# A four-layer conditional block on one core: the dense stage on pairs of tiles as seven block products, the preparation reordered, the adapter tables kept in DRAM

## The reference, cut to what matters

```python
x = x + L0(x)   # long convolution per channel with a kernel made from state space parameters, masked by length
x = x + L1(x)   # einsum('bct,bcd->bdt', x, weights[cond])            weights: (16, 64, 64)
x = x + L2(x)   # x @ base_weight.T + bias + (x @ A[adapter].T) @ B[adapter].T      rank 16 of 32 adapters
x = x + L3(x)   # x @ W.T + 0.5 * (x @ lora_A[labeler]) @ lora_B.T                  rank 32 of 5 labelers
```

## Time and profile before

| | us |
|---|---|
| median of three runs | 1658.99 |
| the profiled execution | 1661.53 |
| its span in the trace | 1659.4 |
| PE busy | 1602.0 (97%) |
| DVE busy | 797.9 (48%) |
| POOL busy | 590.8 (36%) |
| ACT busy | 441.5 (27%) |
| mean granted clock of PE | 0.985 of full speed |

### The profile page before, as it was taken

One profiled execution on the slowest core, in us unless ns is written; L12 is line 12 of the kernel. 1 busy time (PEld: TensorE's weight loads), 2 busy tenths in 40 slices (PEclk: granted clock), 3 DMA queues, 4 the chain that ended last, 5 costly groups with the idle time before them and its releaser, 6 DMA issues.

```text
span 1659.4 us, 32019 instructions
## 1 busy us (share of the span) xinstructions
PE 1602.0 (97%) x10317; PEld 1551.0 (93%) x10317; DVE 797.9 (48%) x1502; ACT 441.5 (27%) x751; POOL 590.8 (36%) x769
## 2 busy tenths in 40 slices
PE   6789989999999998899999999999999999999999
PEld 5678879999999997899999999999999999999998
DVE  7861348878887886233333333333333333333332
ACT  3311134454445543111111111111111111111111
POOL 4552136666666665322222222222222222222221
PEclk9889999999999999899999999999999999999999
DMA  9501357666666764323323232322223223222321
GB/s 239 49 7 56 99 178 243 232 235 238 241 233 228 236 240 170 93 88 100 92 92 99 88 100 92 98 94 92 98 89 98 93 93 98 92 95 92 94 97 65
DMA packets 121309, 214.02 MB, mean 129 GB/s; under 512 B 57873, under 2 KB 74909, under 8 KB 118625
## 3 DMA queue, kind: packets, MB, share of 16 engines
q1 hardware_dynamic: 120988, 213.61, 40.2%
q10 hardware_dynamic: 294, 0.05, 0.0%
HBM read 141.41 MB, written 72.20 MB: 129 GB/s over the span
## 4 chain that ended last, share of the span: by engine, by line
PE 59%; POOL 0%; POOLq 0%; issue 0%; ACT 0%; DVE 0%; DVEq 0%
PE ps L1322 47%; PE ps L1296 7%; PE ps L1344 4%; PE ps L1310 1%; PE ps L1304 0%; POOLq L1151 0%; POOL dense L1172 0%; POOL m_gath L1153 0%; ACT dense L1204 0%; POOLq L1159 0%; POOLq L1158 0%; DVE y_out L1275 0%; POOL a_gath L1162 0%; POOL a_gath L1160 0%; POOL m_gath L1139 0%
## 5 line engine op out<-in xcount | busy, mean ns | idle before, releaser
L1322 PE MATMUL ps<-dense,x2t 128*128 128x384 f32 (+1 forms) x4608 | 821.7, 336 | 0.0
L1322 PEld LDWEIGHTS ps<-dense,x2t 128*128 128x128 f32 x4608 | 775.3, 188 | 2.2
L1172 POOL TENSOR_TENSOR dense<-a_gath,dense 128x384 fp32r<-128x384 f32 x128 | 126.4, 1009 | 499.5 <-ACT dense L1204 499.5
L1007 PE MATMUL ps<-toep,ut 128*128 128x512 f32 (+2 forms) x1152 | 228.2, 343 | 0.0
L1007 PEld LDWEIGHTS ps<-toep,ut 128*128 128x128 f32 x1152 | 195.4, 189 | 16.9
L482 POOL TENSOR_TENSOR toep<-toep_raw,toep 128x1024 fp32r<-128x1024 f32 x64 | 152.5, 2383 | 142.1 <-ACT toep L594 142.1
L1218 ACT ACTIVATE y_out<-ps 128x384 f32<-128x384 f32 x64 | 31.4, 490 | 543.7 <-PE ps L1344 543.7
L1296 PE MATMUL ps<-m_gath,x_in 128*128 128x128 f32 x1024 | 128.3, 280 | 13.4 <-DMA x_in<-x_d 9.6
L1296 PEld LDWEIGHTS ps<-m_gath,x_in 128*128 128x128 f32 x1024 | 123.0, 196 | 13.8 <-DMA x_in<-x_d 9.8
L1250 DVE COPY hm<-ps 64x128 f32<-64x128 f32 x64 | 18.1, 283 | 236.7 <-PE ps L1304 236.7
L905 PE MATMUL ps<-p,staged 128*128 128x512 f32 x528 | 123.1, 395 | 8.9 <-DVE dense L626 8.9
(11 more groups left out here) (184 smaller groups left out, 1726.2 us busy)
## 6 DMA issues: line engine op xcount, KB each, us to landing
toep_raw<-kern_d SPq DMA_DIRECT2D x64, 512.0 KB, 4.2
xt<-in_x SPq DMA_DIRECT2D x64, 512.0 KB, 4.9
x_d<-xt SPq DMA_DIRECT2D x64, 512.0 KB, 4.4
x_in<-x_d SPq DMA_DIRECT2D x64, 512.0 KB, 3.6
out<-y_out SPq DMA_DIRECT2D x64, 512.0 KB, 2.7
stack<-b_d SPq DMA_DIRECT2D x130, 128.0 KB, 2.7
stack<-b_d SPq DMA_DIRECT2D x128, 64.0 KB, 2.7
w_raw<-in_L_cond_W SPq DMA_DIRECT2D x8, 512.0 KB, 7.0
```

The lines of the kernel that those rows point to most:

```text
L1007: mm(y[:, half * HB + i * P:(half + 1) * HB], xs[:, a, half * half_t + i, :], tp[:, b, 0:HB - i * P], start=i == a == b == 0, stop=False)
L1172: ins = nc.gpsimd.tensor_tensor(to[:, 1], of, f(to[:, 0]), ALU.subtract)
L1322: ins = mm(outs[g], x2t[v][:, a, i, :], w[:, b, i % half_t, first:end], start=i == a == b == 0, stop=g == 2 and i == K8 - 1 and a == 1)
```

## The change

Three things change.

**The dense stage works on pairs of tiles.** The two tiles of a pair are the two block rows of a 2 x 2 block matrix, the halves of T its block columns; the dense matrix is cut in four 512 x 512 quadrants. Seven products of 512-deep blocks take the place of eight (Winograd's form of Strassen's method). The operands on the x side (a11, a12, a22 and the sums s1 to s4) are made anew for each pair by ACT and DVE; those on the weight side are made once, in the preparation, by DVE and ACT, by sums of quadrants. Four of the products are wide: they carry the 96 adapter columns. A product is 4 chunks x 3 passes, each as two matmuls: 256 and 256 columns, or 256 and 352 columns. The results lie in six PSUM banks; what two results share is accumulated once and read in between. The two tiles' outputs are put together from several PSUM reads.

**Adapter tables.** The tables of adapter columns are no longer in SBUF. The preparation stores them in DRAM (`a2_d`, `a3_d`) and SP loads the rows of each sample: `tab2` and `tab3`, two DMAs a sample, 128 partitions x 512 or 1024 bytes each. DVE makes for the second tile of a pair the difference of the table's halves (`difference`), ACT and DVE the high and low parts.

**The preparation's jobs are reordered.** After d0 and d4 come layer 3's tables, three of the four B jobs, the small products, the convolution kernels and the transposes of layer 2's A; then d1, d5, d2, d6, d3, d7, and the last B job around the transpose of the first channel. The bias row is loaded by ACT's queue at the start. SBUF is laid out anew. The convolution's instructions stay as they are.

The core of the diff:

```diff
@@ preparation: order of PE's jobs
+    ORDER = [(f"t{i}", 1 + i % 3) for i in range(K8)] + [
+        ("d0", 0), ("par", 1), ("d4", 3), ("a3a", 2), ("a3b", 1), ("b2_0", 0), ("b2_1", 3), ("b2_2", 2),
+        ("c", 1), ("row", 0), ("b3", 3), ("k0", 2), ("k1", 1), ("la0", 0), ("la1", 3), ("la2", 2), ("la3", 1),
+        ("d1", 0), ("d5", 3), ("d2", 2), ("d6", 0), ("d3", 1), ("d7", 2), ("b2_3", 3)]
...
@@ dense stage, SP (sync)
+            def pair(n, last_one):
+                if not last_one:
+                    sp.wait_ge(mixed, 4 * n + 4)
+                    for v in range(2):
+                        load_x1(n + 1, v)
+                    a, l = ids(n + 1, B), ids(n + 1, 2 * B)
+                    for v in range(2):
+                        sp.wait_ge(h_lo[v], n + 1)
+                        load_tables(v, a, l)
+                    sp.wait_ge(adapted, 2 * n + 2)
+                    for v in range(2):
+                        load_c(v, a, l)
+                sp.wait_ge(y12_added, n + 1)
+                sp.dma_start(out_rows[bass.ds(2 * n, 1)].squeeze(0), y_out[0][:]).then_inc(y_stored[0], 16)
+                if not last_one:
+                    sp.wait_ge(p_done, n + 1)
+                    for v in range(2):
+                        load_stack(v, a)
+                sp.wait_ge(y21_added, n + 1)
+                sp.dma_start(out_rows[bass.ds(2 * n + 1, 1)].squeeze(0), y_out[1][:]).then_inc(y_stored[1], 16)
...
@@ dense stage, DVE (vector)
+            def difference(n):
+                dve.wait_ge(tab_landed[1], 64 * n + 64)
+                for t in (tab2[1], tab3[1]):
+                    tt(t[:, :, K4:K8], t[:, :, K4:K8], t[:, :, 0:K4], ALU.subtract).then_inc(diffed, 1)
...
+            def pair(n, last_one):
...
+                if not last_one:
+                    difference(n + 1)
+                dve.wait_ge(m2_done, n + 1)
+                h_rows(n, 0)
+                if not last_one:
+                    h_low(n + 1, 0)
+                h_columns(n, 0)
+                dve.wait_ge(m4_done, n + 1)
+                h_rows(n, 1)
...
+                dve.wait_ge(rv_done, n + 1)
+                tt(halves(y_out[0][:, HB:T]), halves(y_out[0][:, HB:T]), of_r, ALU.add).then_inc(y12_added, 1)
+                dve.wait_ge(p_done, n + 1)
+                tt(halves(y_out[1][:, HB:T]), halves(y_out[1][:, HB:T]), of_p, ALU.add).then_inc(y22_added, 1)
+                tt(halves(y_out[1][:, 0:HB]), halves(y_out[1][:, 0:HB]), of_v, ALU.add).then_inc(y21_added, 1)
...
@@ dense stage, PE (tensor)
+            def turn(n, v):
+                pe.wait_ge(hrow_ready, 2 * n + v + 1)
+                ready(pe, hs_lo, 2 * n + v)
+                nc.tensor.transpose(acc[:, SMALL_BANK, 0:P], hrow[v][:], ident[:]).then_inc(turned, 1)
...
+            def pair(n, last_one):
+                pe.wait_ge(a11_lo, n + 1)
+                pe.wait_ge(h_lo[0], n + 1)
+                ready(pe, y22_added, n)
+                product(xa11, M1, PS_SHARED, P_OWN, ALL, True).then_inc(m1_done, 1)
...
+                product(xs1, M5, RV_SHARED, R_OWN, ALL, True).then_inc(m5_done, 1)
...
+                product(xa12, M2, PS_SHARED, S_OWN, ALL, True).then_inc(m2_done, 1)
...
+                product(xa22, M4, RV_SHARED, V_OWN, FRONT, True)
+                turn(n, 0)
+                product(xa22, M4, RV_SHARED, V_OWN, BACK, True).then_inc(m4_done, 1)
+                adapters(n, 0)
+                quarter(n + 1, 0)
...
+                product(xs2, M6, PS_SHARED, P_OWN, FRONT, False)
+                turn(n, 1)
+                product(xs2, M6, PS_SHARED, P_OWN, BACK, False)
...
+                low_rank(0, 0, acc[:, S_OWN, RIGHT], acc[:, PS_SHARED, RIGHT]).then_inc(lr11_done, 1)
+                adapters(n, 1)
+                quarter(n + 1, 1)
...
+                product(xs4, M3, RV_SHARED, R_OWN, ALL, False)
+                quarter(n + 1, 2)
...
+                product(xs3, M7, PS_SHARED, P_OWN, ALL, False).then_inc(m7_done, 1)
+                low_rank(0, HB, acc[:, RV_SHARED, LEFT], acc[:, R_OWN, LEFT])
...
+                low_rank(1, 0, acc[:, V_OWN, RIGHT], acc[:, RV_SHARED, RIGHT]).then_inc(rv_done, 1)
+                pe.wait_ge(u3_copied, n + 1)
+                low_rank(1, HB, acc[:, PS_SHARED, LEFT], acc[:, P_OWN, LEFT]).then_inc(p_done, 1)
+                quarter(n + 1, 3)
```

More of the change, by code:

```diff
@@ L92, in program, with f, wide @@
[L92 to L96, removed]
+    def f(ap):
+        return ap.bitcast(F32)
+    weights, o_fixed = at("weights", [P, 4, BLOCK], F32R, 0)
+    o_w = [4 * BLOCK * i for i in range(4)]
+    def wide(i, half, m):
+        start = (half * 4 + m) * WIDE
+        return weights[:, i, start:start + WIDE]
@@ new lines, in plain, with quadrant @@
+    def plain(i, half, m):
+        start = 8 * WIDE + (half * 3 + m) * HB
+        return weights[:, i, start:start + HB]
+    def quadrant(i, half, m):
+        return wide(i, half, m)[:, D_AT[m]:D_AT[m] + HB]
+    raw_m5, raw_m4, raw_m6, raw_m7 = [], [], [], []
+    for i in range(4):
+        for raws, start in ((raw_m5, (4 + M5) * WIDE + D_AT[M5]), (raw_m4, (4 + M4) * WIDE + D_AT[M4]),
+                            (raw_m6, 8 * WIDE + (3 + M6) * HB), (raw_m7, 8 * WIDE + (3 + M7) * HB)):
+            raws.append(at(f"raw{start}_{i}", [P, HB], F32, o_w[i] + 4 * start)[0])
@@ L110, in program @@
     bias_p3, o = at("bias_p3", [P, K8], F32, o)
[L112 to L133, removed]
+    o = o_w[0]
     def nat(name, cols, dtype=F32, parts=C):
@@ L180, in program @@
[L180 to L189, removed]
+        t, o = at(name, shape, dtype, o)
+        return t
+    xa11, xs1, xa12, xa22 = (place(n, [P, 2, K4, P], F32R) for n in ("xa11", "xs1", "xa12", "xa22"))
@@ L909, in split_job, with chunk_of @@
                 ins.then_inc(job_done, 1)
+            def chunk_of(t, n, c):
+                for half in range(2):
+                    cols = slice(half * HB, (half + 1) * HB)
+                    for a, b in PASSES:
+                        ins = mm(t[:, cols], staged[n % 2][:, a, c, :], p3[:, c, b, cols],
+                                 start=c == a == b == 0, stop=c == K8 - 1 and a == 1)
+                return ins
             def transpose_w3(i):
-                t = job(J_W3 + i)
+                t = job(f"t{i}")
                 pe.wait_ge(w3_ready, i + 1)
@@ L1070, in program @@
+    y11_added, y12_added, y22_added, y21_added = (sem(f"{n}_added") for n in ("y11", "y12", "y22", "y21"))
     PAIRS = TILES // 2
@@ L1224, in _ @@
+            over_pairs(act, pair)
         @block.vector
@@ new lines, in h_rows @@
+            def h_rows(n, v):
+                own, other = ((P_OWN, H_END), (S_OWN, H_FRONT)) if v == 0 else ((R_OWN, H_END), (V_OWN, H_FRONT))
+                parts = []
+                for b in range(2):
+                    rows, cols = slice(b * C, (b + 1) * C), slice(b * R2, b * R2 + R2 + R3)
+                    parts.append((hrow[v][rows, cols], rows, slice(b * (R2 + R3), (b + 1) * (R2 + R3))))
+                first, second = acc[:, own[0], own[1]], acc[:, other[0], other[1]]
+                for b, (to, rows, cols) in enumerate(parts):
+                    ins = nc.vector.tensor_copy(to, first[rows, cols])
+                ins.then_inc(h_part, 1)
+                dve.wait_ge(h_part, 2 * n + v + 1)
+                for to, rows, cols in parts:
+                    ins = tt(to, to, second[rows, cols], ALU.add)
+                ins.then_inc(hrow_ready, 1)
@@ L1347, in tile, with quarter @@
-            def tile(k, v):
-                if exists(k, v + 1):
-                    mixing(k, v + 1)
-                dense(k, v)
-            mixing(0, 0)
-            over_tiles(pe, tile)
+            QUARTERS = ((0, 0), (1, 0), (1, 1), (0, 1))
+            def quarter(n, q):
+                v, half = QUARTERS[q]
+                if half == 0:
+                    pe.wait_ge(x1_landed[v], 16 * n + 16)
+                    pe.wait_ge(gathered[v], n + 1)
+                ready(pe, quarter_read, 4 * n + q)
+                for i in range(K4):
+                    c = half * K4 + i
+                    ins = mm(acc[:, MIX_BANK, i * P:(i + 1) * P], x1_in[v][:, c * P:(c + 1) * P], m_gath[v][:], start=True, stop=True)
+                ins.then_inc(mixed, 1)
```

1205 lines of the change are left out of this document (670 added, 535 removed).

## The result

The changed kernel takes 1870.61 us (median of 4 runs, 1869.19 to 1873.19) against 1659.37 us for the kernel before on the same chip: ratio 1.1273 [1.1253, 1.1292]. It is slower, as predicted; the prediction said 1925 us, 54 us too many. The span is 1868.5 us, the mean granted clock 0.933.

A forecast was written before the change was run, and what follows sets the result against it. PE alone bound the old kernel; the new bound is a ring through SP (19.1 us), DVE (1.9), PE (14.9) and y12's add (1.0): 36.9, with 2.5 clock loss 39.4 a pair. With start, end and preparation: 1925 us, range 1800 to 2010.

The forecast's parts named there:

- SP was to be never idle for long: Dense stage, SP's queue: a sign that would show the prediction right; no size beyond these words.
- PE's leg: PE from turn 0 to `rv_done` in a pair: 14.9 us of work, plus 2.5 us of lost clock.
- the ring: Dense stage: y12 added, SP's loads, DVE, turn 0, PE, y12 added; 39.4 us a pair with clock loss, chance 0.70.
- rival 1: Dense stage: tables land in time, 9.9 us after y12's add, and PE is the bound; 1590 us, chance 0.12.
- two x1 loads and eight reads: SP's queue before the table loads: 0.9 us for the loads and 6.4 (5.7 to 8.4) for the `value_load`s.
- landing: Table rows arriving after SP's last table load: 2.8 us, 2.7 as the stack's 128 KB, up to 3.6 as x1.
- DVE from landing to the transpose: DVE's `difference` and four small `h_rows` copies with hand-overs, before turn 0: 1.9 us.
- clock loss: PE behind 9 us of idle time before each turn 0: 2.5 us more a pair, bounds 0 and 3.
- rival 2: Dense stage: the tables' wait holds in each pair but PE's clock stays up; 1850 us, chance 0.10.
- Rival 3: SP's queue: released at the mixing's end rather than by y12's add; 1780 us, chance 0.05.
- Rival 4: PE's seven products don't save, 256-column pairs costing more in alternating banks; 10% more is +45 us, chance 0.02.
- The 0.4 us for which M1 was to wait for y22's add: Pair's end: `y22_added` comes 1.7 us after `rv_done`, next M1 due at 1.3; costs only if tables don't hold PE.

The follow-up runs named there:

- e2: The changed kernel with each pair's eight stack loads issued by GpSimd instead of SP: 1806.2 us, ratio 1.088.
- e3: The changed kernel with SP's eight reads of table numbers made twice in each pair: 2009.88 us, ratio 1.2107.
- e4: The changed kernel with 44 unused 256-column matmuls added on PE before turn 0 in each pair: 1839.91 us, ratio 1.1083.
- e8: The changed kernel with 56 unused 256-column matmuls added on PE before turn 0 in each pair: 1820.91 us, ratio 1.0980.
- e1_late: The changed kernel with the next pair's table work moved behind this pair's adapter copies on VectorE and behind two reads on ScalarE: 1594.37 us, ratio 0.9609.
- e5_dve: The changed kernel with only `difference` moved, on VectorE, behind `h_columns(n, 1)`; ScalarE's order kept: 1835.85 us, ratio 1.1071.
- e9_dve2: The changed kernel with `difference` and `h_low(n + 1, 0)` both moved behind `h_columns(n, 1)` on VectorE, ScalarE's order kept: 1666.93 us, ratio 1.0028.

## Why the prediction was right, and where it was off

The mechanism is the one named, and the marks of the wait are there: DVE idle before `difference`, released by the table DMA (12.0 us, 8 to 10 were said); PE idle in front of the transpose, 31 times as said, 30 of them 7.1 us and one of 2.2 in pair 0; a granted clock well below 1 in a pair. One mark failed: SP was to be never idle for long, and it waits 17 us in each pair:

```profile
SPq L1211 <- PE ps L1503: 367.0, 31, 12.2
```

These 11.8 us a pair stand between the last table load and the loads of the small matrices, and 5.2 us more in front of the store of y12. They run beside PE's leg and so change nothing in the ring's length, but they are room: the eight reads for the next pair could stand there. No run tried it.

Each edit of the ring's own terms (e2, e3, e4, e8) moves the time by about what the ring's length says, and taking VectorE and ScalarE out of it gives the time of rival 1, whose sum was 1590 us and which e1_late makes 1594.37.

The surplus of 55 us is in the ring's terms. Start and end fit: the first transpose was to come at 701.4 - 6 = 695.4 and came at 692.9; from the transpose of pair 30 to the end of the span it was 48.4 and is 48.5. The median is 2.1 us over the span, where 0.4 below it was taken. That the convolution ended 5 us earlier than before (652.7 against 657.9), where 6 were said, proves little: in the nine traces that share this preparation its end lies between 651.5 and 658.4. The ring was 39.4 and is 37.57, and 30 x 1.83 = 55. Term by term:

| step of the ring | predicted | measured |
|---|---|---|
| store and eight stack loads | 4.45 | 1091.90 - 1087.04 = 4.86 |
| store of y_out1 and turn of the loop | 0.95 | 1.04 |
| two x1 loads and eight reads | 7.3 | 6.40 |
| seven steps of table loads | 3.5 | 3.61 |
| landing | 2.8 | 2.10 |
| DVE from landing to the transpose | 1.9 | 1.47 |
| PE's leg to y12's add, with clock loss | 14.9 + 0.3 + 2.5 = 17.7 | 1086.18 - 1069.00 = 17.2 |
| y12's add and SP's wake | 0.8 | 0.86 |

The reads were the largest miss: 5.5 us where 6.4 were said, below the lower bound of 5.7 taken from GpSimd. The 6.4 us gave the first two reads 2.1 us, from a gap on SP behind a store. SP's records in that gap show nothing but the two reads and their register work, but the reads themselves took 0.67 and 0.54 us there, where in the changed kernel the first takes 0.45 and the others 0.26 to 0.28; why they are slower behind a store is not shown. The 1.43 us for each further two are an idle time of GpSimd that also holds the register work of the copies behind; two reads are 1.29 on SP. The Trainium skill (DMA: Bandwidth & Descriptors, "Latency and other measured facts") puts a `tensor_load` at about 600 ns at least; the 4.8 us made of it was nearer to the 5.5 than mine, but the second set of e3_reads, at 0.55 us from one read to the next, lies below that floor, and the measurement decides. The landing was read from the stack's DMA of the same size; the tables' own takes 2.1 us. DVE's steps follow each other closer than their durations (0.55 us from `difference` to the first copies, 0.45 to the next). The clock loss was taken from the preparation, behind idle times of 8 to 9 us; here the wait is 7.1 us and the loss 1.8. Store and stack loads went the other way, 0.4 us over what was said.

The granted clock came down in each pair, as it does behind the idle stretches of the preparation, and rival 2 (the clock stays up because the idle time is regular) is out: its 1850 us would have been 1821, the e8_warmer time. The Trainium skill (TensorE: Matmul & The Clock Gate, "HAM oscillation — how this bites in real kernels") describes that a wait in each step makes the loss recur at each step; the trace agrees, at 1.8 us of 37.6.

The granted clock of a pair is 0.91, not 0.85, which had been said for a longer wait and a larger loss. Rival 3 (SP is released by the mixing's end) is out: the x1 loads start 1.0 us behind the second store (1091.90, 1092.94), and before the first store SP waits 5.2 us for y12's add. Rival 4 (the products don't save) is out too: in the changed kernel a 256-column matmul starts 0.12 us before the next one (680.85 and 680.97, at full clock), as taken from the earlier trace rows, and e1_late's pair of 28.35 us of PE work stands beside the 28.1 predicted. The 0.4 us for which M1 was to wait for y22's add is not there: all of PE's idle time in a pair of e1_late is 0.1 us.

What the prediction did not see is the second and third wait behind the first. It named `difference` alone. e5_dve shows that the change could not be mended there: `h_low(n + 1, 0)` ahead of `h_columns(n, 0)` holds PE nearly as long, and behind it ScalarE's `h_high` ahead of its take makes a ring of 30.5 us (e9_dve2, 30.75 on average). Rival 1 as it was put, with the tables landing 9.9 us after y12, was not needed: e1_late leaves SP's 18 us as they are and moves the ones who wait.

## What to carry over

When a step for the next round stands in an engine's queue ahead of a copy that the busiest engine waits for now, follow the data of that step to the queue that loads them and back to what releases it. If this closes a ring, its length, not the engines' work, is the time of a round. To mend it, move the waiting step behind everything that this round needs, on each engine that has one. In this kernel, with only the one that the profile names moved, 35 of 276 us came back, because the next one on the same data took over.

## What was unexpected

- PE's clock fell in pairs of e4_warm in which PE had waited only 1.8 to 2.1 us (2.1 before the 0.50 in 952 to 954), while other pairs with the same work and waits of up to 2.05 us kept 1.00.
- With work moved to another queue, both got slower: with GpSimd issuing the stack loads beside SP, the landing of the stack loads went from 3.9 to 5.5 us, of x1 from 5.2 to 8.8, of the tables from 2.1 to 2.5, and two x1 issues took 1.37 instead of 0.88 us.
- A read of a table number costs SP 0.65 us with its address work when it stands behind other reads (0.55 when the address is there already); eight of them (5.5 us with the step to the first) cost a pair more than the eight stack loads (4.3 us).
